# Gated delta-rule attention, experts, SSD and a folded butterfly FFN on one core: the recurrence in chunks of four steps in place of eight

## The reference

```
q, k = l2norm(silu(conv4(silu(x @ W + b))));  v = silu(conv4(silu(x @ Wv + bv)))
a, bt = sigmoid(x @ Wa.T + ba), sigmoid(x @ Wb.T + bb)        # per head
step over 256 tokens, state S of 8 x 8 per batch and head:
    S = a*S - a*bt * (S k) k^T + bt * v k^T
    o = q^T S
out = O @ Wo.T + bo
```

## Time and profile before

| | |
|---|---|
| three runs | 560.89, 563.94, 565.34 us; median 563.94 |
| the profiled execution | 564.0 us, span from first to last instruction 561.9 us |
| PE busy | 464.7 us (83%) |
| ACT busy | 392.8 us (70%) |
| DVE busy | 378.4 us (67%) |
| POOL busy | 188.4 us (34%) |
| mean granted clock of TensorE | 0.936 |

### The profile page before, as it was taken

How to read it: one execution, slowest core, us unless ns; L and a number is a source line. 1 busy time by engine, 2 the same in 40 slices (tenths; PEclk the granted TensorE clock), 3 DMA queues, 4 the chain that set the end, 5 groups by cost and what they waited for, 6 DMA issues and landing times.

```text
span 561.9 us, 6536 instructions
## 1 busy us (share of the span) xinstructions
PE 464.7 (83%) x2110; PEld 312.2 (56%) x2110; DVE 378.4 (67%) x665; ACT 392.8 (70%) x661; POOL 188.4 (34%) x188
## 2 busy tenths in 40 slices
PE   3695696678966978999998989999997998997079
PEld 2584572566744765666675555667664576652023
DVE  1247878898779999789998976999414176111820
ACT  4777867776798548888746997665998757754243
POOL 0243651576145963048970105332002000011001
PEclk9977897879978999899998999999999999998779
DMA  7636793032440311800320081000000000000000
GB/s 195 245 105 171 226 309 97 18 102 69 121 89 1 94 39 58 189 2 1 95 76 0 1 193 37 0 2 0 1 1 20 0 2 0 1 19 0 1 1 19
DMA packets 35761, 36.49 MB, mean 65 GB/s; under 512 B 12936, under 2 KB 30992, under 8 KB 35472
## 3 DMA queue, kind: packets, MB, share of 16 engines
q1 hardware_dynamic: 35440, 31.88, 21.9%
q10 hardware_dynamic: 288, 4.19, 2.0%
HBM read 31.61 MB, written 3.28 MB: 62 GB/s over the span
## 4 chain that ended last, share of the span: by engine, by line
PE 40%; ACT 27%; DVE 19%; issue 9%; POOL 2%; DMA 2%; SPq 1%; DVEq 0%; ACTq 0%; POOLq 0%
PE psF L761 9%; PE psS L779 9%; ACT hid L1325 4%; ACT L1131 4%; ACT L1129 4%; DVE U L1861 3%; DVE T L1863 3%; DVE T L1859 3%; PE psB L718 2%; ACT hS L1174 2%; PE psA L593 2%; PE psM L822 2%; PE psF L836 2%; ACT sq L1159 2%; PE psM L829 1%
## 5 line engine op out<-in xcount | busy, mean ns | idle before, releaser
L779 PEld LDWEIGHTS psS<-we2s,hid 128*128 128x128 f32 x1024 | 137.7, 198 | 61.5 <-issue 42.6
L761 PE MATMUL psF<-h,we1s 128*128 128x512 f32 (+1 forms) x320 | 142.7, 540 | 12.7 <-ACT hid L1325 11.7
L779 PE MATMUL psS<-we2s,hid 128*128 128x128 f32 x1024 | 141.0, 283 | 8.6 <-ACT hid L1325 5.5
L1325 ACT ACTIVATE hid<-psF,col 128x512 f32<-128x512 f32 (+1 forms) x160 | 93.2, 600 | 55.7 <-PE psF L761 54.9
L761 PEld LDWEIGHTS psF<-h,we1s 128*128 128x128 f32 x320 | 56.7, 203 | 42.7 <-ACT hid L1325 21.4
L2253 POOL TENSOR_TENSOR QS<-H,qn 128x512 f32<-128x512 f32 x32 | 49.1, 1548 | 58.0 <-DVE H L1869 58.0
L1882 DVE SCALAR_TENSOR_TENSOR acc<-psS,gate,acc 128x128 f32<-128x128 f32 x128 | 36.1, 341 | 45.5 <-PE psS L779 45.5
L1869 DVE TENSOR_TENSOR_SCAN H<-A,T 128x576 f32<-128x576 f32 x32 | 55.1, 1721 | 1.1
L1131 ACT ACT_TABLE_LOAD x42 | 53.9, 1283 | 1.4 <-PEq L2402 0.7
L1861 DVE TENSOR_REDUCE U<-T 128x64 f32<-128x576 f32 x32 | 38.6, 1205 | 1.1
L1129 ACT ACT_TABLE_LOAD x30 | 38.5, 1283 | 0.5
(11 more groups left out here) (198 smaller groups left out, 777.1 us busy)
## 6 DMA issues: line engine op xcount, KB each, us to landing
wrep<-scratch_dram SPq DMA_DIRECT2D x64, 144.0 KB, 3.5
krep<-scratch_dram SPq DMA_DIRECT2D x64, 128.0 KB, 3.0
hid<-fold_mats_dram SPq DMA_DIRECT2D x22, 256.0 KB, 3.6
we1s<-we_dram ACTq DMA_DIRECT2D x1, 2048.0 KB, 10.1
we2s<-we_dram ACTq DMA_DIRECT2D x1, 2048.0 KB, 17.4
wrep<-XX SPq DMA_DIRECT2D x8, 144.0 KB, 3.6
outT_dram<-x SPq DMA_DIRECT2D x4, 256.0 KB, 2.6
scratch_dram<-XX SPq DMA_DIRECT2D x3, 288.0 KB, 2.1
```

Source lines behind the costliest of these rows:

```text
L761: mm(bank[name][:, 0:ncols(w)], we1s[:, e, k * P:(k + 1) * P], h2[w % 2][:, 0:ncols(w)], start=True, stop=True).then_inc(s_hid_mm, 1)
L779: last = mm(bank[name][:, t * P:(t + 1) * P], hid[n % 2][:, k, t * P:(t + 1) * P], we2s[:, e, k, :], start=(k == 0), stop=(k == HT - 1))
L1325: nc.scalar.activation(hid[x_ % 2][:, k, 0:c], psF[n % 2][:, 0:c], ACT.Silu, bias=pc("be1", HT * e + k)).then_inc(s_hid_done, 1)
```

## The change

Chunks have four steps: `CH = 4`, so 64 chunks, `C9 = 5`, and three elimination steps (`STEPS`) and two groups of key products (`PACKS`) per window; the waits that counted 7 and 4 per window count these. `T9` and `U` become views of one PSUM bank, `psT`, which takes the place of `psA`; `psA` becomes the bank of `X1`. `A9` and `H` have eight buffers each. The scratch in DRAM is gone: SP reads `kn` and `XX` in SBUF directly, each source partition going to the 8 partitions of its head by one DMA per channel e; POOL, before it writes `kn` or the keys of `XX` again, waits for all these DMAs of the window before. The order on every engine is written anew: among other things `convolve(2)` stands ahead of `ln(("moe", 0))` on DVE, and `center` of a coming window stands later on PE, closer to the call that frees its bank; of the 23 fills eight (three before) stand ahead of `experts_back(4)`.

```diff
-CH = 8
+CH = 4
-PACK = [(0, 6), (1, 5), (2, 4), (3,)]
+PACK = [(0, 2), (1,)]
+STEPS = CH - 1
+PACKS = len(PACK)
...
-        NA = 4
+        NA = 8
-        U = sb("U", P, NB, CH)
-        T9 = sb("T9", P, DH + 1, NB, C9)
-        NH_ = 4
+        NH_ = 8
...
-        psA = pb("psA", P, COLS)
+        psT = pb("psT", P, COLS)
+        T9 = psT[:, 0:(DH + 1) * NB * C9].rearrange("p (e b i) -> p e b i", e=DH + 1, b=NB)
+        U = psT[:, COLS - NB * CH:COLS].rearrange("p (b i) -> p b i", b=NB)
         psM = pb("psM", P, 2, COLS)
+        psA = psM[:, 1, :]
...
             def spread_keys(w):
-                n = ncols(w)
                 sp.wait_ge(s_kn_done, w + 1)
-                sp.dma_start(scratch[w, 0, :, 0:n], kn[:, 0:n]).then_inc(s_kn_out, 16)
-                sp.wait_ge(s_kn_out, 16 * (w + 1))
                 for i, h in enumerate(halves(w)):
                     if h > 1:
                         sp.wait_ge(s_outer_done, CPH * (h - 1))
-                    for d in range(DH):
-                        sp.dma_start(krep[h % 2][d::DH, :, :], scratch[w, 0, :, i * HC:(i + 1) * HC].rearrange(
-                            "(h e) n -> h e n", e=DH)).then_inc(s_krep_in[h % 2], 16)
+                    for e in range(DH):
+                        sp.dma_start(krep[h % 2][:, e, :], kn[e::DH, i * HC:(i + 1) * HC].unsqueeze(1).broadcast_to(
+                            [HEADS, DH, HC])).then_inc(s_krep_in[h % 2], 16)
             def spread_solved(w):
...
-                sp.dma_start(scratch[w, 1, :, 0:n // CH * C9], XX[:, 1, 0:n // CH, :].rearrange("p g i -> p (g i)")).then_inc(s_xk_out, 16)
-                sp.wait_ge(s_xk_out, 16 * (w + 1))
...
+                    for e in range(DH):
+                        sp.dma_start(wrep[h % 2][:, e, :], XX[e::DH, 1, at:end, :].rearrange("p g i -> p (g i)").unsqueeze(1).broadcast_to(
+                            [HEADS, DH, H9])).then_inc(s_wrep_in[h % 2], 16)
...
             def center(key):
...
-                free("A")
+                free("X1")
                 mm(psA[:, 0:k], cst("center"), src, start=True, stop=True).then_inc(s_ln_c, 1)
-                read["A"] = s_ln_n1, n + 1
+                read["X1"] = s_ln_n1, n + 1
...
             def modulation():
                 pe.wait_ge(s_fold_in, 64)
+                free("X1")
...
             def decay_products(n):
...
-                if n > 0:
-                    pool.wait_ge(s_xk_out, 16 * n)
+                for h in (halves(n - 1) if n > 0 else ()):
+                    pool.wait_ge(s_wrep_in[h % 2], 16 * DH * (h // 2 + 1))
             def keys(n):
...
-                if n > 0:
-                    pool.wait_ge(s_kn_out, 16 * n)
+                for h in (halves(n - 1) if n > 0 else ()):
+                    pool.wait_ge(s_krep_in[h % 2], 16 * DH * (h // 2 + 1))
...
             begin()
             first_modulation()
             ln(("front", 0))
-            carry_hf(1)
             biases()
             convolve(0)
+            carry_hf(1)
+            ssd_halo(0)
+            ln(("front", 1))
             modulation()
-            ln(("front", 1))
+            carry(1)
             couple(0, 0)
             couple(0, 1)
-            carry(1)
-            couple(0, 2)
-            couple(0, 3)
             solve(0)
             carry_hf(2)
+            ln(("front", 2))
             convolve(1)
+            for i in range(0, 4):
+                chunk(0, i)
             carry(2)
-            ln(("front", 2))
-            for i in range(0, 3):
+            for i in range(4, 8):
                 chunk(0, i)
             couple(1, 0)
-            chunk(0, 3)
-            for i in range(1, 4):
-                couple(1, i)
+            couple(1, 1)
             solve(1)
+            convolve(2)
             ln(("moe", 0))
-            convolve(2)
```

More of the change, by code:

```diff
@@ L1372, in _ @@
             modulate(("front", 0))
+            projected(0, 0)
+            projected(0, 1)
             ln_square(("front", 1))
-            for i in range(0, 3):
-                projected(0, i)
+            projected(0, 2)
             first_taps(0)
             projected(0, 3)
+            projected(0, 4)
+            ln_scale(("front", 1))
+            convolved(0)
+            modulate(("front", 1))
+            norms(0)
+            decays(0, 0)
+            projected(1, 0)
+            projected(1, 1)
@@ L1451, in _ @@
             hidden(0, 3, 3)
+            decays(2, 1)
             ln_scale(("front", 3))
+            norms(2)
             hidden(0, 4, 0)
-            hidden(0, 4, 1)
             modulate(("front", 3))
-            decays(2, 1)
-            hidden(0, 4, 2)
-            hidden(0, 4, 3)
-            projected(3, 0)
-            hidden(0, 5, 0)
+            for i in range(1, 4):
+                hidden(0, 4, i)
+            hidden(0, 5, 0)
+            decays(2, 2)
+            decays(2, 3)
+            hidden(0, 5, 1)
@@ new lines, in _ @@
+            decays(2, 7)
+            decays(2, 8)
+            hidden(0, 7, 1)
+            decays(2, 9)
+            hidden(0, 7, 2)
+            hidden(0, 7, 3)
+            routed(1)
+            route_exp(1)
+            for i in range(0, 3):
+                hidden(1, 0, i)
+            gate_rows(1)
+            hidden(1, 0, 3)
+            hidden(1, 1, 0)
+            projected(3, 4)
+            router_bias(1)
+            hidden(1, 1, 1)
+            ln_square(("front", 4))
+            hidden(1, 1, 2)
@@ L1502, in _ @@
+            hidden(1, 1, 3)
+            for i in range(0, 4):
+                hidden(1, 2, i)
+            decays(2, 10)
+            hidden(1, 3, 0)
+            hidden(1, 3, 1)
+            for i in range(11, 14):
+                decays(2, i)
+            hidden(1, 3, 2)
+            convolved(3)
             attn_branch(2)
-            hidden(1, 3, 1)
-            ln_scale(("front", 4))
-            hidden(1, 3, 2)
+            decays(2, 14)
+            decays(2, 15)
             hidden(1, 3, 3)
@@ L1507, in _ @@
             hidden(1, 4, 0)
+            ln_scale(("front", 4))
+            norms(3)
             hidden(1, 4, 1)
-            decays(2, 7)
             hidden(1, 4, 2)
+            decays(3, 0)
             hidden(1, 4, 3)
-            decays(3, 0)
-            for i in range(0, 4):
-                hidden(1, 5, i)
             modulate(("front", 4))
+            decays(3, 1)
+            hidden(1, 5, 0)
+            hidden(1, 5, 1)
+            for i in range(2, 5):
+                decays(3, i)
@@ L1605, in _ @@
+            decays(4, 6)
             ffn_out(0)
-            router_bias(3)
             hidden(3, 1, 1)
             hidden(3, 1, 2)
-            decays(4, 4)
+            decays(4, 7)
             hidden(3, 1, 3)
+            for i in range(8, 11):
+                decays(4, i)
             hidden(3, 2, 0)
+            hidden(3, 2, 1)
+            router_bias(3)
+            hidden(3, 2, 2)
+            hidden(3, 2, 3)
+            decays(4, 11)
             ln_square(("ssd", 1))
+            hidden(3, 3, 0)
@@ L2063, in _ @@
[L2063 removed]
+            for i in range(3, 6):
+                mix_expert(0, i)
             convolve(3)
[L2065 removed]
             ln(("moe", 1))
+            for i in range(0, 4):
+                chunk(2, i)
+            route(1)
+            chunk(2, 4)
             mix_expert(0, 6)
[L2068 to L2071 removed]
+            up_bias()
+            chunk(2, 5)
+            mix_expert(0, 7)
+            chunk(2, 6)
```

859 lines of the change are left out of this document (415 added, 444 removed).

## The result

The changed kernel takes 559.84 us (median of 15 runs, 558.46 to 563.07) beside 563.47 for the kernel before on the same chip: a ratio of 0.9927, 95% interval 0.9898 to 0.9956. It is faster by 4 us, where 21 were forecast. The profiled execution has a span of 557.0 us (before 561.9) and a mean granted clock of 0.94.

A forecast was written before the change was run, and what follows sets the result against it. It took the chain through window 0 to bound up to 94 us, DVE and PE nearly tied to 400, then PE. 564.0 - 6 (start) - 12 (middle) - 2 (PE) = 544, rounded to 543; range 533 to 553.

The forecast's parts named there:

- the middle term: 94 to 400 us: DVE work falls by 24 us, half of it, 12, reaches the end; bounds 0 and 24.
- PE leads, DVE is close behind: Reading of 233 to 400 us before the change: PE busy 156.8 of 167 us, DVE 147.8.
- the forecast's PE term (2): PE: key products 6.5 us less, five more fills ahead of the experts' end; 2 us gained.
- The start, -6: Up to the first expert product: shorter elimination, no DRAM copy, fewer POOL products; 6 us gained, bounds 0 and 12.
- The chunk: DVE's four chunk instructions: two four-step chunks take 4.9 to 5.3 us against 5.05; 2 us more in all.
- rival (d): DVE writes T9's PSUM bank slowly, 31 us, eating the gain: 557; 19% together with (b).
- Elimination and coupling: DVE's solve and coupling per window: elimination 46.6 to 17.6 us, coupling 7.5 us less; together 36 us less.
- (a): DVE is the real pacemaker up to 400 us, so all 24 us pass: 526; chance 20%.
- (b): PE's list order paces the middle, DVE only waits longer; start and PE gains remain: 557; 19% with rival (d).
- (c): `center` takes X1 and PE stands until DVE reads it, 4.4 us at eight norms: 578; chance 11%.

## Why the prediction was wrong

**What failed is the middle term:** "of a stretch where each of two engines is the later one about half the time I take half, 12". From the first expert product to the router of window 4 the kernel won 3.3 us (307.5, before 310.9) where 12 were forecast. The solve alone, 18 us shorter in the old lists, paid 3.4 us; the sum, 15 us shorter in the new ones, nothing. Behind 233 us PE's own work is the pace (0.6 us for each), and DVE's 147.8 of 167 us in the earlier trace rows are high without holding PE back, as PE's waits show. "PE leads, DVE is close behind" was read from busy shares, and as an order of the two it holds; what a shorter DVE is worth had to be read from the waits. That leaves 94 to 233 us, where the short solve in the old lists does win time and the changed kernel does not. There the new lists put the keys behind a layer norm. That this placement is what took the gain was not shown: moving the third window's keys ahead brought 1 to 2 us. The 2.0 us won behind 402 us are the size of the forecast's PE term (2); what brought them was not tested.

**The start, -6, was 0.** The solve shrank as said (43.10 to 46.1 us, 3.0 against my 2.8), and the copy to DRAM is gone. But the first keys are late: PE runs `modulation()` ahead of `square_sums(0)` and waits 5.2 us for X1 until the second window's norm has been read.

```profile
22.89 4.38 PE L612 MATMUL psM<-csil,wrep 128*128 128x8 f32 x20 [5.18 <-DVE hf L1779]
27.12 2.05 PE L641 MATMUL psS<-norm,C 128*128 128x256 f32 x4
...
40.14 1.22 PE L652 MATMUL psS<-zb,C 128*128 128x256 f32 x2 [5.43 <-POOL zb L2260]
```

The first solve starts at 43.1, not at 40.87, the first chunk at 55.34 and not near 51, and the first expert product at 94.59 against 94.12. I had named `fold(2)` as the call that the bank would hold; it was `modulation()`, and with it the keys. Two moves in the lists brought 2 us back.

The first chunk still starts 2.3 us earlier than before (57.66, now 55.34), and its half is done earlier too. Nothing of that reaches the norm of the experts. POOL's last products for the half, and PE's attention output, before and after:

```profile
78.16 1.21 POOL L2253 TENSOR_TENSOR QS<-H,qn 128x512 f32<-128x512 f32 x1 [1.29 <-DVE H L1869]
...
81.89 3.62 PE L718 MATMUL psB<-QS,worep 128*128 128x256 f32 x16
```

```profile
72.74 4.31 POOL L2277 TENSOR_TENSOR QS<-H,qn 128x256 f32<-128x256 f32 x6
...
81.78 3.61 PE L713 MATMUL psB<-QS,worep 128*128 128x256 f32 x16
```

POOL is done at 79.4 before and at 77.1 after, and PE runs the output at 81.9 and 81.8, both times without a wait: it stands behind the folding and the projections of the third window in PE's list. The forecast took the 1.10 us of the earlier trace rows as a sign that DVE's list and the attention were tied; the way through the attention was PE's list, which a lighter recurrence does not shorten.

**The chunk** was right: 615, 565, 427 and 825 ns forecast, 623, 466, 428 and 820 measured. The one miss is the sum, which came near its lower bound of 450 (the contiguous rate of the earlier trace rows) and not to the middle. The relief of scan and outer product, for which no row existed, came in full, and writing to PSUM cost next to nothing (the first product's median is 541 ns, and 533 with the tile in SBUF): rival (d) is out. The errata section of "VectorE: DVE Perf Modes" in the Trainium skill would add, as an estimate from its figures, some 65 ns for each instruction with a PSUM source. It is not borne out here either: 428 ns with the PSUM operand against a median of 426 from SBUF.

**Elimination and coupling**: 20.4 us against 17.6, since the steps of 256 elements take some 550 ns (427 forecast) and the subtraction of 768 takes 1223 (957 forecast); coupling went from 11.2 to 5.2, 6.0 against 7.5. POOL's two groups fell by 35 us (32 forecast), PE's key products from 16.0 to 7.7, ACT's copies are 24.3 (27). The sizes on DVE and ACT mattered little, as the slopes show; PE's counts for more, but is small.

**The rivals.** (a), DVE the pacemaker, is refuted by the two shortenings. (b), the order paces the middle and DVE waits longer for it, comes nearest to what happened; it had 19% with (d). That its 557 (by its own terms 556) lies so near the 560 measured is in part luck: it counts 6 us from the start, which did not come, and nothing from the middle, which brought 3.3. (c), the shared bank, is real but was priced by holds of 4.4 us each: the whole bank costs 4.5 us in the SBUF form. PE's waits for readers of X1 that a layer norm put there come to 11.6 us in all. Whether the bank acts through them or through where the keys then have to stand in the lists, no run separates.

**What stays open.** The kernel is as fast as before up to 233 us although its lists were laid for lighter work; the two placements that were moved, the first and the third window's keys, are worth 4 to 6 us together. Which others cost, and how much a full new layout would give, was not tried. Nor is it shown what part of the 14 us that chunks of four cost in the old lists is the chunk; the tiles in PSUM don't fit with chunks of eight (648 of 512 columns).

## What to carry to other kernels

When lists are fixed by hand or by a planner, the price of longer work says little of the gain from shorter work: here the padded solve cost 0.8 us for each us in one kernel, and cutting it in the other paid 0.2. Before half of an engine's saving is counted, read for each stretch what the fullest engine waits for: its waits for the lightened engine (here 5 us of 272) say what to expect, and its whole idle time (17.6) is the most that can go while its own work stays. A wait for a third engine can still go back to the lightened one. When an earlier result is to pay, look whether its reader is waiting for it at all, or is busy with what stands ahead in its own list. When two users come to share a buffer, look for the chain that the new order puts behind it, and not for the wait alone.

## What the hardware showed that was not expected

A sum over nine parts at a long stride, 288 elements, takes 698 ns from SBUF and 466 from PSUM, with a spread of 25 ns in the one and 1 in the other. A contiguous one from SBUF would take 450, as an estimate by the rate of the earlier trace rows, so in PSUM this stride costs next to nothing. With the tiles in SBUF one execution of the scan reached 1777 ns beside a median of 825 while POOL worked; with one source in PSUM all 64 took 820, though POOL worked as before, and the one product of the chunk that kept two sources in SBUF still went up to 1159 ns. POOL gained too: its reads of the state take 827 ns where they take 900 with the tiles in SBUF.
